# Where an image's output strips are stored, where TensorE's image loop jumps back, and in which round the tail taps stand

## The reference

```
x = x + irfft2(complex 3x3 conv(rfft2(gn(x))) + bias)    layer 0, done without an FFT
x = x + gate(gn(x)) * gn(x)                               layer 1: a channel pair's row is kept or zeroed
x = x + conv3x3(gn(x), W)                                 layer 2, zero padding 1
x = x + conv3x3(gn(x), weight)                            layer 3, zero padding 1
```

## Time and profile before

| | |
|---|---|
| three runs | 4857.66, 4846.31, 4855.79 us; median 4855.79 |
| the profiled execution | 4858.67 us, span 4856.9 us |
| PE busy | 4578.8 us (94%), 84784 matmul records |
| DVE, ACT busy | 2924.3 us (60%), 2482.2 us (51%) |
| mean granted clock of PE | 0.965 |
| DMA | 468.15 MB, mean 96 GB/s |
| instruction transfers (queue q8) | 525 packets, 8.60 MB |

### The profile page before, as it was taken

One profiled execution on the slowest core, in us unless ns is written; L12 is line 12 of the kernel. 1 busy time (PEld: TensorE's weight loads), 2 busy tenths in 40 slices (PEclk: granted clock), 3 DMA queues, 4 the chain that ended last, 5 costly groups with the idle time before them and its releaser, 6 DMA issues.

```text
span 4856.9 us, 222294 instructions
## 1 busy us (share of the span) xinstructions
PE 4578.8 (94%) x84784; PEld 2919.9 (60%) x84784; DVE 2924.3 (60%) x10604; ACT 2482.2 (51%) x7085; POOL 3.2 (0%) x14
## 2 busy tenths in 40 slices
PE   5999999999999999999999999999999999988898
PEld 1555765556655666556655566555665556655566
DVE  2677717776277762777537774377734777257770
ACT  4555455544555445554455544555445554544435
POOL 0000000000000000000000000000000000000000
PEclk8999999999999999999999999999999999999999
DMA  6443036420364113541145411464014540233104
GB/s 193 114 123 93 6 80 177 141 74 17 93 176 138 54 26 105 174 129 44 32 113 167 129 36 36 116 178 124 24 40 132 168 119 19 51 112 106 54 4 142
DMA packets 290071, 468.15 MB, mean 96 GB/s; under 512 B 25393, under 2 KB 92145, under 8 KB 289265
## 3 DMA queue, kind: packets, MB, share of 16 engines
q1 hardware_dynamic: 289392, 458.29, 33.5%
HBM read 323.98 MB, written 134.22 MB: 94 GB/s over the span
## 4 chain that ended last, share of the span: by engine, by line
PE 92%; issue 3%; DVE 3%; ACT 1%; SPq 1%; ACTq 0%; DVEq 0%; DMA 0%
PE ps L1248 35%; PE ps L1168 19%; PE ps L1153 18%; PE ps L1161 6%; PE ps L1177 5%; PE ps L1027 5%; PE ps L1273 1%; PE ps L1073 1%; PE ps L1074 0%; PE ps L1100 0%; PE ps L1222 0%; PE ps L1300 0%; PE ps L1115 0%; ACT shared L491 0%; ACT x L566 0%
## 5 line engine op out<-in xcount | busy, mean ns | idle before, releaser
L1248 PE MATMUL ps<-x,conv_s 32*32 32x512 f32 x49104 | 1716.2, 602 | 21.9 <-issue 21.9
L1248 PEld LDWEIGHTS ps<-x,conv_s 32*32 32x32 f32 x49104 | 1229.5, 103 | 476.6 <-issue 234.6
L566 ACT ACTIVATE x<-ps,vec 128x256 f32 (+1 forms) x1024 | 490.6, 494 | 1017.9 <-PE ps L1168 1017.9
L817 DVE COPY vsb<-ps 128x512 f32<-128x512 f32 x512 | 329.7, 685 | 1128.3 <-PE ps L1153 1128.3
L1168 PE MATMUL ps<-hil,shared 128*128 128x256 f32 x4096 | 994.7, 386 | 0.0
L1168 PEld LDWEIGHTS ps<-hil,shared 128*128 128x128 f32 x4096 | 741.3, 191 | 274.6 <-issue 194.6
L805 DVE SCALAR_TENSOR_TENSOR shared<-xin,trig 128x256 f32<-128x256 f32 x2048 | 821.7, 440 | 57.5
L632 ACT ACTIVATE x<-ps,vec 64x512 f32<-64x512 f32 (+1 forms) x768 | 525.5, 684 | 424.7 <-PE ps L1248 414.4
L1153 PE MATMUL ps<-shared 32*32 32x512 f32 x16384 | 669.0, 614 | 3.8 <-issue 3.8
L623 ACT ACTIVATE x<-ps,vec 128x512 f32 x512 | 347.2, 684 | 467.9 <-PE ps L1248 467.9
L1153 PEld LDWEIGHTS ps<-shared 32*32 32x32 f32 x16384 | 309.0, 104 | 295.0 <-issue 231.8
(11 more groups left out here) (170 smaller groups left out, 2713.2 us busy)
## 6 DMA issues: line engine op xcount, KB each, us to landing
xin<-x SPq DMA_DIRECT2D x512, 256.0 KB
out<-x SPq DMA_DIRECT2D x512, 256.0 KB
shared<-x SPq DMA_DIRECT2D x448, 256.0 KB, 4.1
shared<-t_strip SPq DMA_DIRECT2D x512, 96.0 KB, 3.6
x<-x SPq DMA_DIRECT2D x64, 256.0 KB, 5.2
x<-t_proj SPq DMA_DIRECT2D x1, 2048.0 KB, 10.7
hil<-t_hil SPq DMA_DIRECT2D x1, 560.0 KB, 11.0
trig<-t_trig SPq DMA_DIRECT2D x1, 512.0 KB, 11.0
```

The lines of the kernel that those rows point to most:

```text
L566: ins = nc.scalar.activation(split_in(strip_of(s))[:, q, :], split_in(ps[:, bank, :])[:, q, :], ACT.Identity, bias=v1(MEAN), accum_out=sum ...
L817: V.tensor_copy(vsb[:, e, :], ps[:, BV + e, :]).then_inc(v_copied, 1)
L1248: mm = pe.matmul(ps[TM * cg:TM * cg + TM, banks[k], :], conv_s[TM * rg:TM * rg + TM, kw, second, :], x1[TM * rg:TM * rg + TM, of, kw:kw + ...
```

## The change

Three edits, all of order; no arithmetic is added or taken away.

```diff
-DEFERRED = STRIPS // 2
+DEFERRED = STRIPS - 2 * UNROLL
...
                 for pair in range(DEFERRED // 2):
                     feed(pair, 2 * pair % TABLES)
                     if stores_left:
                         for e in range(2):
                             store(i - 1, STRIPS - DEFERRED + pair * 2 + e)
-                with sp.Fori(DEFERRED // 2 // UNROLL, PAIRS // UNROLL - 1) as j:
-                    for k in range(UNROLL):
-                        feed(j * UNROLL + k, 2 * k)
                 for pair in range(PAIRS - UNROLL, PAIRS):
                     feed(pair, 2 * pair % TABLES)
...
                 for n in range(PAIRS):
-                    if more:
+                    if more and n >= PAIRS - (STRIPS - DEFERRED):
                         sp.wait_ge(evicted, ev(i, 1 + STRIPS + 2 * n + 2))
                         sp.sem_inc(s_sp, 1)
-                        store(i, n)
-                    else:
+                        store(i, n - (PAIRS - (STRIPS - DEFERRED)))
+                    elif not more:
                         for e in range(2):
                             store(i, 2 * n + e)
...
-                for kw in range(TAPS):
-                    mm = pe.matmul(ps[0:TM, BTAIL, :], conv_s[TM:2 * TM, kw, 0, :], x1[TM:2 * TM, STRIPS - 1, kw:kw + N], start=(kw == 0), stop=(kw == TAPS - 1))
-                mm.then_inc(convolved, 1)
+                def tail_tap(kw):
...
+                    if kw == TAPS - 1:
+                        mm.then_inc(convolved, 1)
...
                         taps(n, PAIRS - 1 - n, banks2(n), outputs2, 0, kw)
+                        if n == 0:
+                            tail_tap(kw)
...
-            with pe.Fori(0, B - 1) as i:
-                image(i, True)
-            image(B - 1, False)
+            first_layer(0, True)
+            with pe.Fori(0, B - 2) as i:
+                convolutions(i, True)
+                first_layer(i + 1, True)
+            convolutions(B - 2, True)
+            first_layer(B - 1, False)
+            convolutions(B - 1, False)
```

More of the change, by code:

```diff
@@ L1126, in _, with due, first_layer @@
             column_sums(0)
-            def image(i, more):
+            def due():
+                pe.sem_inc(pair_due, 1)
+            def first_layer(i, more):
                 t0 = i * STRIPS
                 u0 = i * (STRIPS // UNROLL)
-                def due():
-                    pe.sem_inc(pair_due, 1)
                 def mix(t, odd):
@@ L1226, in image, with convolutions @@
                 project_next(2, TABLES - 2, PAIRS // 2 - 1, False)
+            def convolutions(i, more):
                 pe.wait_ge(v_part, i + 1)
@@ L1271, in image @@
                 due()
-                for kw in range(TAPS):
-                    mm = pe.matmul(ps[0:TM, BTAIL, :], conv_s[TM:2 * TM, kw, 0, :], x1[TM:2 * TM, STRIPS - 1, kw:kw + N], start=(kw == 0), stop=(kw == TAPS - 1))
-                mm.then_inc(convolved, 1)
+                def tail_tap(kw):
+                    mm = pe.matmul(ps[0:TM, BTAIL, :], conv_s[TM:2 * TM, kw, 0, :], x1[TM:2 * TM, STRIPS - 1, kw:kw + N],
+                                   start=(kw == 0), stop=(kw == TAPS - 1), skip_group_check=True)
+                    if kw == TAPS - 1:
+                        mm.then_inc(convolved, 1)
                 for slot in range(PAIRS * TAPS + LAG2):
```

## The result

| | median | runs |
|---|---|---|
| before | 4853.93 us | 6 (4846.31 to 4857.66) |
| changed | 4803.61 us | 6 (4789.18 to 4815.76) |

The ratio is 0.99 (95% interval 0.9881 to 0.9918): the changed kernel is 40 to 58 us faster. I had forecast 4830, 28 us faster, with a range down to 4811. The direction is right, the size is not, and the time lies outside the range.

What follows compares the result with a forecast made beforehand. PE was taken to bound the kernel (92% of the path), losing time to instruction fetches at jumps and block ends. Gains of 45.8 us less costs of 17.5 left 28.3, from 4858.67 to 4830 us; range 4811 to 4852.

Steps and rivals of the forecast that it cites:

- Part 3: Block ends move: image 0's falls behind the edge-term matmuls, 2.1 us gained; the idle stays in images 1 to 6.
- Part 4: Third convolutions: with 24 of 32 strips' stores moved to the first layer, 12.2 us of fetch idles go (5 to 20).
- Part 2: Statistics before the second convolution: the jump arrives there five times at 2.3 us, costing 11.5 us, plus 2 for clock.
- rival B: First layer: stores delay loads or instruction fetch, 0.5 us per step costs 42 us, 4872 us; chance 0.07.
- Part 5: Second convolution's start: spread tail taps overlap nothing and the first tap waits for three gates; costs 4 us (-10 to 6).
- the 2 us that I charged to the jump: Start of the second convolution: clock lost through the longer idle in the statistics, 2 us in all (0 to 5).
- Part 1: Image boundary, third convolution's end to third mix: the jump leaves it, 31.5 us gained (21 to 39).
- SP's jump: Boundaries before images 2 to 6: SP's own unmoved loop jump delays a load of x, third mix at about 20.1 us.
- Rival D: More gain from boundary, late third-convolution idles and tail taps: 4812 us; chance 0.11.
- DVE's detour at no cost: Image boundary: waiting for DVE's copies behind the late strip costs nothing, 7.5 us more gain.
- overlapping tail taps: Start of second convolutions: spread tail taps run beside other taps, 4 us more gain.
- The signs: Profile marks named beforehand as showing the forecast right or wrong, at boundary, statistics, third convolution and first layer; no size.

Runs made afterwards that it cites:

- b_pad80: Kernel before plus 80 semaphore increments at the start of PE's program, moving all later code: 4828.0 us against 4850.7, ratio 0.9957.
- a_pad180: Changed kernel plus 180 semaphore increments at the start of PE's program: 4819.2 us, ratio to before 0.9936.
- x_def: Kernel before with the store change alone (56 strips stored in the next first layer), PE's program untouched: 4821.8 us against 4851.9, ratio 0.9945.
- y_rot3: Changed kernel with the jump moved on, between second and third convolution: 4809.1 us, ratio to before 0.9911.
- x_tail: Kernel before with the spread tail taps alone: 4853.5 us against 4851.9, ratio 1.0005.
- y_notail: Changed kernel with the tail taps back in one run ahead of the first pair: 4801.0 us, ratio to before 0.9898.
- b_pad256: Kernel before plus 256 semaphore increments at the start of PE's program, one block more: 4869.1 us, ratio 1.0035.
- z_defpad: Kernel before with the deferred stores and 80 increments at the start, image loop not turned: 4809.1 us, ratio 0.9923.
- y_two: Changed kernel with two images per round of PE's loop, so two jumps taken instead of five: 4794.8 us, ratio to before 0.9888.
- x_rot: Kernel before with PE's turned image loop alone, stores and tail taps as before: 4820.7 us against 4851.9, ratio 0.9940.
- z_pad255: Changed kernel plus 255 increments at the start, so each jump lands on a block's last instruction: 4828.4 us, ratio to before 0.9956.

## Why the prediction was wrong

The direction came from the right reasons; parts 3 and 4 and a term that the sum did not have carry the error. Against the sum of 4830.4 the profiled execution is 26.8 us faster. By stages, the gain over what was forecast is 14.8 us in the third convolutions (part 4), 9.9 in mixes 3 to 17 (no term), 6.2 from E to partner sum (parts 2 and 3 together) and 1.1 to the second convolution's end, less 1.6 at the boundary and 3.6 at the start.

**Part 3 failed.** "In images 1 to 6 it still lies inside (offset 277 instead of 353 of 384), so the idle stays." The block's end does lie there, but the block before begins at instruction 21 instead of 97. I asked where a block ends; what counts is when the sequencer enters it against when it leaves it. Shown by b_pad80 and a_pad180, which do nothing else: 2.1 us of idle predicted to go, 13 went (13.3 to 0.4).

**Part 4's term was mis-sized.** 12.2 us predicted; 27.0 in this pair of profiles, 24.8 in x_def, and 19.6 between the means of the five kernels with all stores (964.8) and the nine with deferred ones (945.2). "The last eight pairs keep their stores and their idles" failed: six of the thirteen idles from 0.7 us were there, and x_def, with the same code, has one left (0.92 us). What I took for idles spread over all blocks are every eighth fetch, three or so per third convolution, and the late half of them went as well. The 27.0 us are the seven idles that I had counted (8.7), 6.5 of the 7.7 us of idle in the last eight pairs, 3.2 in image 7, whose stores are as before, and 8.6 beside the recorded idles, for which I had 3.5. Why the last pairs lose theirs though they still store is not shown; in a_pad180 some are back. That the first layer bears the stores held: no step from the third mix on takes more than 10.3 us, and rival B is out.

**Part 2 was mis-sized, against me.** 2.3 us a jump predicted, 3.4 to 4.4 measured, 18.5 in all for 11.5. I had taken 3.7 us for a branch without stores; it takes 4.3 where it meets the fetch in order, 3.4 where it does not (a_pad180). It also starts 2.1 us after the first E matmul and not 4.2 ("about 1046.2"), since nothing inside them stops it any more: part 3's idle had hidden a piece of it. The clock: second convolutions of images 2, 4 and 5 begin at half clock (1.2 GHz) and take 111.7 to 112.1 us; images 0 and 3 take 105.7. Windows over the first four pairs of images 0 and 4 (PEclk behind the counts):

```profile
475.63:485.63 10.00, 10.00 (x202) 4.79 (x204) 8.84 (x25) 0.92 (x3) 0.00 (x0) 1.00 0.01 2
...
2816.54:2832.54 16.00, 16.00 (x192) 5.52 (x202) 8.78 (x25) 0.77 (x2) 0.00 (x0) 0.61 0.01 1
```

Six us, then, for an image that is caught. But y_rot3 without a jump there has three such images and one of 110.7, and x_tail two (111.6). What these kernels share are the spread tail taps: second convolutions above 111 us are found in five of the six kernels that have them (15 images of 48) and in none of the eight with the tail taps in one run (at most 110.2). So this cost goes with part 5's edit rather than with the jump; by what way is not shown, and the 2 us that I charged to the jump stand neither proved nor refuted.

**Part 1 held in size.** 31.5 us predicted, 29.9 in this pair, 23 between the means of all profiles: the kernel before happened to be profiled with its longest boundaries. Its working held too. The third load of x comes late as computed, DVE takes it at 12.5 us after the convolution's end (I had 12.7):

```profile
1307.23 0.49 DVE L798 TENSOR_SCALAR xin<-xin,vec 128x512 f32<-128x512 f32 x1 [4.90 <-DMA xin<-x]
```

Ahead of images 2, 3, 5 and 6 the copy that the turn behind the second mix needs is ready 15.7 to 16.0 us after the end (I had 16.1), and the turn's weight load waits for it, 0.4 to 1.9 us; plainest ahead of image 3, at full clock (the convolution ends at 1884.80):

```profile
1900.57 0.75 PE L1174 MATMUL ps<-eye,vsb 128*128 128x128 f32 x4 [1.51 <-DVE vsb L814]
```

Third mixes come at 19.7 to 20.2 us; I had 20.1. Ahead of images 1 and 4 it is PE's own work, at half clock for 6.8 us, that sets the 20.2: the copy is ready before. So image 1, without SP's jump, did not come to 18.6; y_notail's, at full clock, took 17.9.

**Part 5 held within its error.** 4 us of cost predicted; x_tail 2 (-3 to 7), and y_notail one us faster than the changed kernel by the ratios. Its working is half right. The wait for the gates grew from 12.2 to 17.6 us over the eight images, as computed; but in six images of x_tail the stretch from partner sum to the second convolution's end is still 0.2 to 1.3 us shorter, where I had it longer. In the other two it is 3.9 and 4.3 us longer, with the half clock.

**The hitches were missing from the sum.** In mixes 3 to 17 the kernel before loses 10 us, which the change gives back. They are late fetches too: 5 us of them in image 4 (fetch 272, a multiple of 8 again), in x_def and x_tail as well, whose code lies as before; b_pad256 has 6 in image 3 (fetch 207), one image earlier, like its other idles. It is not the turn that cures them: b_pad80 and z_defpad, unturned and moved by 80, have none either. Of the turned kernels y_rot3 has one of 3.5 and a_pad180 one of 1.8 us. So they too hang on the place of the code. The sum had no term for them.

**The sum by stages**: 29.9 + 9.9 + 27.0 in gains; 3.2 (E), 4.9 (to the second convolution's end) and 3.6 (the start, where loads vary) in costs; 55.1 of the spans' 55.2. Rival D, at 0.11, had one of the missing parts: the late idles of the third convolution, for 6 us. Its other two, DVE's detour at no cost and overlapping tail taps, did not bring what it said.

**The signs.** Held: the boundary stretches, the wait for DVE's copy behind a load of x, DVE's wait of about 2.3 us for the partner sum (2.51), no taps' idle in the first 24 pairs of images 0 to 6. Not held: branches of 3.3 to 4.2 us (4.3 to 4.6), and E without idle in image 0 alone.

## What to carry to other kernels

Where "issue" idles remain in a long program, count where its blocks of 256 instructions begin against the stretches that issue fastest, and against its jumps: here 80 instructions of filler gave 21 us, against 27 and 29 for the two edits, and every edit of the code moves it, so a test of an edit is also a test of that place. Pad the start and measure both before crediting an edit. Put a jump back over much code where the engine waits for others anyway, and let it land on a block's start.

## What the runs showed of the hardware

- Increments of a semaphore at the start take about 0.16 us each (40.9 us for 256), so that 80 are covered by a wait of 14 us. 160 and 180 start the first matmul 11 to 14 us later but not the first mix; 256 cost 12 us.
- A taken branch of TensorE over some 16,500 instructions takes 3.3 to 3.7 us in the statistics where no other fetch starts near it (a_pad180), 3.8 to 4.0 with one that starts 0.3 to 0.4 us ahead of it (y_two), 4.2 to 4.8 with one that starts up to 0.6 us behind it (changed, x_rot, y_notail, z_pad255), and 3.3 more where it lands on a block's last instruction (z_pad255). At the image boundary, alone, it took 3.3 to 4.1 us.
- Of every eight fetches of TensorE's code one or two neighbours start 1.4 to 2.0 us later than the others while a third convolution stores half an image (67 to 69 GB/s over the stretch in the kernel before; also in x_tail, x_rot and b_pad256), and none does in second convolutions (4 GB/s). Which of the eight differs between kernels.
